# Attention rows written straight into the output projection's input buffer, and the expert scatters spread over seven steps

## The reference

```python
x = x + _layernorm(attn_ref(_layernorm(x), ...))
x = x + _layernorm(ffn_ref(_layernorm(x), ...))
# attn_ref, at its end:
scores = jnp.where(causal, -jnp.inf, einsum('bhqd,bhkd->bhqk', q, k) * scale)
out = einsum('bhqk,bhkd->bhqd', softmax(scores), v)
out = out.transpose(0, 2, 1, 3).reshape(b, s, E)
return out @ wo + bo
# ffn_ref: shared expert of every row, plus w[:, e] * expert e for the top 2 of 8
```

## Time and profile before

| | |
|---|---|
| median of 3 runs | 858.82 us (854.71 to 861.81) |
| the profiled execution | 860.77 us, its span 859.0 us |
| PE / PEld busy | 673.4 / 330.8 us (78% / 39%) |
| DVE / ACT / POOL busy | 611.7 / 502.0 / 322.8 us (71% / 58% / 38%) |
| DMA | 70.38 MB in 110289 packets, 45136 of them under 512 bytes |

### The profile page before, as it was taken

One profiled execution on the slowest core, in us unless ns is written; L12 is line 12 of the kernel. 1 busy time (PEld: TensorE's weight loads), 2 busy tenths in 40 slices (PEclk: granted clock), 3 DMA queues, 4 the chain that ended last, 5 costly groups with the idle time before them and its releaser, 6 DMA issues. The chain is left out here.

```text
span 859.0 us, 17320 instructions
## 1 busy us (share of the span) xinstructions
PE 673.4 (78%) x6080; PEld 330.8 (39%) x6111; DVE 611.7 (71%) x1244; ACT 502.0 (58%) x1048; POOL 322.8 (38%) x437
## 2 busy tenths in 40 slices
PE   5876289999898898988898998795486799989800
PEld 2332023333342242332242343232364677777600
DVE  6999498888878979868979878851246256555466
ACT  3663066777768786768776778684253234444323
POOL 3775012222222331742331742323612436465632
PEclk9998589999999999999999999998687999999955
DMA  5456261121222212422222431012521235232182
GB/s 147 138 171 179 61 165 37 23 53 49 57 52 53 74 53 55 96 70 41 74 62 46 121 71 29 21 54 58 177 74 38 70 87 154 75 84 67 44 226 73
DMA packets 110289, 70.38 MB, mean 82 GB/s; under 512 B 45136, under 2 KB 96753, under 8 KB 110207
## 3 DMA queue, kind: packets, MB, share of 16 engines
q1 hardware_dynamic: 97356, 56.34, 26.4%
q0 software_dynamic: 4352, 8.99, 3.1%
q10 hardware_dynamic: 8498, 3.97, 1.8%
HBM read 40.21 MB, written 26.56 MB: 78 GB/s over the span
## 5 line engine op out<-in xcount | busy, mean ns | idle before, releaser
L1145 ACT ACTIVATE expT<-ps 128x512 f32<-128x512 f32 (+1 forms) x640 | 324.9, 557 | 129.6 <-PE ps L1373 124.4
L303 DVE TENSOR_REDUCE block_max<-ps 128x8 f32<-128x1024 f32 x288 | 340.3, 1218 | 61.8 <-PE ps L288 43.1
L1346 PE MATMUL ps<-expT,vr 128*9 128x256 f32 (+1 forms) x2560 | 180.1, 363 | 17.2 <-ACT oT L1118 14.8
L1373 PE MATMUL ps<-q_space,k_space 64*128 64x512 bf16 (+3 forms) x768 | 164.1, 335 | 10.2 <-DMA q_space<-negT 6.7
L288 PE MATMUL ps<-k_space,q_space 64*128 64x128 bf16 (+3 forms) x1152 | 132.7, 281 | 34.6 <-DVE block_max L303 24.3
L1106 POOL TENSOR_SCALAR_AFFINE_SELECT expT<-expT 128x512 f32<-128x512 f32 x128 | 82.4, 656 | 195.2 <-ACT expT L1145 195.1
L1373 PEld LDWEIGHTS ps<-q_space,k_space 64*128 64x128 bf16 x768 | 46.2, 94 | 150.7 <-ACT expT L1145 99.7
L1555 POOL DMA_INDIRECT expert_rows<-row_ring,tile_to x72 | 68.9, 957 | 69.0 <-ACT row_ring L1639 46.9
L1346 PEld LDWEIGHTS ps<-expT,vr 128*9 128x9 f32 x2560 | 42.3, 89 | 99.3 <-issue 47.5
L715 POOL DMA_INDIRECT sorted_rows<-rows,places x64 | 63.2, 988 | 42.9 <-DVE places L900 25.1
L288 PEld LDWEIGHTS ps<-k_space,q_space 64*128 64x128 bf16 x1152 | 49.7, 96 | 73.9 <-DVE block_max L303 58.2
(11 more groups left out here) (200 smaller groups left out, 949.6 us busy)
## 6 DMA issues: line engine op xcount, KB each, us to landing
row_ring<-sorted_rows SPq DMA_DIRECT2D x72, 65.0 KB, 2.0
q_parts<-parts SPq DMA_DIRECT2D x24, 128.0 KB, 2.3
k_parts<-parts SPq DMA_DIRECT2D x24, 128.0 KB, 2.3
q_space<-q_parts SPq DMA_DIRECT2D x32, 96.0 KB
k_space<-k_parts SPq DMA_DIRECT2D x32, 96.0 KB
v_ones<-v_st SPq DMA_DIRECT2D x8, 288.0 KB, 2.7
vr<-v_ones SPq DMA_DIRECT2D x16, 144.0 KB
q_space<-q_parts SPq DMA_DIRECT2D x32, 64.0 KB
```

What stands on the lines that cost most here:

```text
L303: nc.vector.reduce_max(bm[:, g % 2, 2 * f:2 * f + 2, at:at + 4], ps[:, 2 * odd:2 * odd + 2].rearrange("p h (n k) -> p h n k", k=P), AX_X). ...
L1145: act.activation(expT[:, (NS * g + s) % PTN, hh, 0:width], ps[:, B_S + n % S_RING, 0:width], ACT.Exp, scale=SCALE).then_inc(exp_ok, 1)
L1346: last = nc.tensor.matmul(ps[32 * hh:32 * hh + VW, B_O, at:at + n], vr[:, g % RING, kt, hh * VW:(hh + 1) * VW], expT[:, (NS * g + s) % PTN ...
L1373: last = nc.tensor.matmul(ps[:, B_S + n % S_RING, col:col + m], head_rows(kr, g, hh, slice(kt * P, (kt + 1) * P)), head_rows(qr, g, hh, sl ...
```

## The change

The DRAM tensor `attn` and the buffer `att` go. VectorE's multiply writes its four heads' columns straight into the buffer that `turn_at` reads. That buffer is now double by batch: `at_even` for batches 0 and 2, and `at_odd`, which lies in a part of `q_space` that stage two doesn't use, for batches 1 and 3. `turn_at` waits for VectorE's last multiply of the batch instead of the loads, and `load_chunk` loads only the rows of x. The twelve scatters that stood in steps 3 to 6 of groups 8 and 12 are now seven in steps 3 to 6 of these groups and five in steps 3 to 5 of groups 9 and 13. The number of score banks is three in both kernels.

```diff
+SENT = {(0, 3): (4, 2), (0, 4): (6, 2), (0, 5): (8, 2), (0, 6): (10, 1), (1, 3): (11, 2), (1, 4): (13, 1), (1, 5): (14, 2)}
-        at3 = sb(top, "at3", [P, 2, NT, E])
+        at_even = sb(top, "at_even", [P, 2, NT, E])
+        at_odd = q_space[:, 0, GH // 2:].rearrange("p h s -> p (h s)").bitcast(F32).rearrange("p (c t e) -> p c t e", c=2, e=E)
-        AT_DMAS = NG + 1
+        AT_DMAS = 1
+        def at_rows(c):
+            return (at_even, at_odd)[c // 2 % 2][:, c % 2]
+        def att_ready(c):
+            return used_after("out", NG * (c // 2 + 1) - 1, c % 2)
 def load_chunk(sp, c):
             wait(sp, mid_ok, c - 1)
-            for hg in range(NG):
-                sp.dma_start(at3[:, c % 2, :, hg * GH * HD:(hg + 1) * GH * HD], ad[c // 2, hg, c % 2]).then_inc(at_in[c % 2], DMA)
 def turn_at(pe, c, bank):
-            pe.wait_ge(at_in[c % 2], DMA * AT_DMAS * (c // 2 + 1))
+            pe.wait_ge(wide_used, att_ready(c))
 # SP, stage two
-                        for half in range(2):
-                            sp.wait_ge(att_out[half], DMA * NG * (q + 1))
-                            if at == slot and kind == "out":
-                                sp.wait_ge(wide_used, n + 1)
-                                store(gg, which)
-                sp.wait_ge(att_out[0], DMA * G)
                 load_chunk(sp, CHUNKS - 2)
-                sp.wait_ge(wide_used, used_after("out", G - 1, 1))
-                store(G - 1, 1)
-                sp.wait_ge(att_out[1], DMA * G)
                 load_chunk(sp, CHUNKS - 1)
 # GpSimd, stage two: after root(...) of the same step
-                    if q >= 1 and r == 0 and 3 <= s < 7:
-                        for i in range(3 * (s - 3) + 4, 3 * (s - 3) + 7):
-                            scatter(pool, q - 1, i // PAIR_T, i % PAIR_T)
+                    if q >= 1 and (r, s) in SENT:
+                        rows_sent(q - 1, *SENT[r, s])
 # VectorE, "out"
-                        v.reciprocal(rsum[:, which], o[:, :, HD]).then_inc(recip_ok, 1)
-                        wait(dve, att_out[which], DMA * g)
-                        v.tensor_tensor(att[:, which].rearrange("p t (h d) -> p (t h) d", d=HD), o[:, :, 0:HD],
-                                        rsum[:, which].unsqueeze(2).to_broadcast([P, NT * GH, HD]),
+                        v.reciprocal(r, o[:, :, :, HD]).then_inc(recip_ok, 1)
+                        v.tensor_tensor(at_rows(2 * (g // NG) + which)[:, :, cols_of].rearrange("p t (h d) -> p t h d", d=HD),
+                                        o[:, :, :, 0:HD], r.unsqueeze(3).to_broadcast([P, NT, GH, HD]),
                                         ALU.mult).then_inc(wide_used, 1)
```

More of the change, by code:

```diff
@@ L902, in turn_at @@
         def turn_at(pe, c, bank):
-            pe.wait_ge(at_in[c % 2], DMA * AT_DMAS * (c // 2 + 1))
+            pe.wait_ge(wide_used, att_ready(c))
             for t in range(NT):
-                last = nc.tensor.transpose(ps[:, bank, t * P:(t + 1) * P], at3[:, c % 2, t], identf[:])
+                last = nc.tensor.transpose(ps[:, bank, t * P:(t + 1) * P], at_rows(c)[:, t], identf[:])
             last.then_inc(at_turned, 1)
@@ L971, in block_kernel @@
             recip_ok = sem(two, "recip_ok")
-            att_out = [sem(two, f"att_out{h}") for h in range(2)]
             B_S, S_RING, B_O = 4, 3, 7
@@ L995, in load @@
                     load_group(sp, g)
-                def store(g, half):
-                    sp.dma_start(ad[g // NG, g % NG, half], att[:, half]).then_inc(att_out[half], DMA)
                 def place_neg(g):
@@ L1041, in _ @@
                         for p, _, at, kind, gg, which, n in items:
-                            if at == slot and kind == "out":
-                                sp.wait_ge(wide_used, n + 1)
-                                store(gg, which)
-                            elif at == slot and kind == "neg":
+                            if at == slot and kind == "neg":
                                 sp.wait_ge(wide_used, n + 1)
                                 place_neg(gg)
-                sp.wait_ge(att_out[0], DMA * G)
                 load_chunk(sp, CHUNKS - 2)
-                sp.wait_ge(wide_used, used_after("out", G - 1, 1))
-                store(G - 1, 1)
-                sp.wait_ge(att_out[1], DMA * G)
                 load_chunk(sp, CHUNKS - 1)
@@ L1075, in split_neg, with rows_sent @@
                     nc.gpsimd.tensor_scalar(n[2], left[:], -1.0, None, ALU.mult).then_inc(split, 1)
+                def rows_sent(q, first, n):
+                    for i in range(first, first + n):
+                        scatter(pool, q, i // PAIR_T, i % PAIR_T)
                 def side(g, s):
@@ L1089, in side @@
                     if q >= 0 and r == 3 and s >= 8:
-                        for t in (2 * (s - 8), 2 * (s - 8) + 1):
-                            scatter(pool, q, 0, t)
-                    if q >= 1 and r == 0 and 3 <= s < 7:
-                        for i in range(3 * (s - 3) + 4, 3 * (s - 3) + 7):
-                            scatter(pool, q - 1, i // PAIR_T, i % PAIR_T)
+                        rows_sent(q, 2 * (s - 8), 2)
+                    if q >= 1 and (r, s) in SENT:
+                        rows_sent(q - 1, *SENT[r, s])
                 split_neg(0)
@@ L1204, in item @@
                         dve.wait_ge(wide_ready, n + 1)
[L1205 to L1206 removed]
+                        o = ps[:, 2 * odd].rearrange("p (t h w) -> p t h w", h=GH, w=32)
+                        r = rsum[:, which].rearrange("p (t h) -> p t h", h=GH)
+                        v.reciprocal(r, o[:, :, :, HD]).then_inc(recip_ok, 1)
                         dve.wait_ge(recip_ok, 2 * g + which + 1)
[L1208 to L1210 removed]
+                        cols_of = slice(GH * HD * (g % NG), GH * HD * (g % NG + 1))
+                        v.tensor_tensor(at_rows(2 * (g // NG) + which)[:, :, cols_of].rearrange("p t (h d) -> p t h d", d=HD),
+                                        o[:, :, :, 0:HD], r.unsqueeze(3).to_broadcast([P, NT, GH, HD]),
                                         ALU.mult).then_inc(wide_used, 1)
@@ L1584, in norm_proj @@
                 def norm_proj(c):
-                    normalize(act, 0, c, ps[:, B_PROJ[c % 2]].rearrange("p (t e) -> p t e", e=E), at3[:, c % 2], range(NT))
+                    normalize(act, 0, c, ps[:, B_PROJ[c % 2]].rearrange("p (t e) -> p t e", e=E), at_rows(c), range(NT))
                 A, Z = CHUNKS - 2, CHUNKS - 1
```

10 lines of the change are left out of this document (4 added, 6 removed).

## The result

The changed kernel took **851.9 us** (median of 20 runs, 845.1 to 857.1), the kernel before 858.85 us (20 runs, 854.71 to 863.92). The ratio is 0.9915, 95% interval 0.9896 to 0.9934. That is 7.0 us faster, and 5.7 to 8.9 us by the interval. The forecast was 10.6 us. The two profiled executions do differ by 10.7 us (860.77 and 850.1), as the sum over one profile had said. The medians do not.

A forecast was written before the change was run, and what follows sets the result against it. TensorE was taken to set stage two's pace, with the DRAM trip costing at its reload waits and the stage's end. 4.6 + 5.6 + 0.4 = 10.6 us off the 858.8 median gave 848.2 us, range 843.5 to 853.0.

The forecast's parts named there:

- The wait of `turn_at`: Groups 8 and 12: TensorE's waits for the reload and the clock loss behind one go, 4.6 us gained, lower bound 0.
- rival (b): Stage two: another wait takes the reload's place, only the 6.0 us of the stage's end remain, 852.8 us; chance 0.10.
- The scatters: GpSimd, groups 8, 9, 12, 13: moved scatters cost nothing, with 2.0 us of slack before group 9's split.
- The multiply: VectorE's multiply in its new write form: cost taken as 0, bounded by 9.3 us, with 2 us kept for the range.
- SP's queue: SP in stage two: 32 stores and 32 loads go, nothing waits on the moved loads; costed at nothing.
- The end of the stage: End of stage two: SP no longer last, GpSimd's DRAIN ends it, stage three starts at 598.0; 5.6 us gained.
- The bound of 7.8 us: End of stage two: upper bound of the gain, if VectorE's end decides when stage three starts.
- (a): End of stage two: GpSimd's DRAIN, lengthened by contention with SP's transfers, doesn't hold it; 2.2 us earlier, 846.0 us; chance 0.12.
- (e): End of stage two gives nothing, SP being held elsewhere: 854.2 us; chance 0.04.
- The start of stage three: First rows come sooner by 0 to 2 us; only ScalarE's wait for the first down product counts, 0.4 us.
- Rival (c): TensorE's clock falls differently after the shorter gap: 1.5 us a stretch, two make 851.2 us; high side's chance 0.08.

The follow-up runs named there:

- the down weights first: The kernel before with SP's down weight loads ahead of its last store and reload (chunk 7): 858.85 us, ratio 0.9981.
- scatters alone: The kernel before with only the new places of the twelve scatters, attention rows still through DRAM: 861.82 us, ratio 1.001.
- the kernel without late scatters: The changed kernel with group 15's four scatters moved to the start of stage three, second chip: 879.87 us, ratio 0.9861 to the kernel before.
- the kernel with early roots: The changed kernel, stage three's four roots between and right behind its scatters, ahead of the row numbers: 875.76 us (second chip), 847.93 us (third).

## Why the prediction was right, and where it was off

The sum of waits, by trace, in us. The kernel before has three traces: the first, the one on the third chip, and the one with the scatters moved (which changes nothing that can be told). The changed one has four: the first, two more, and the one with the scatters moved back.

| | before | after | mean difference |
|---|---|---|---|
| group 8 | 31.41, 28.62, 31.04 | 27.84, 27.84, 27.84, 27.97 | -2.5 |
| group 12 | 29.09, 28.89, 28.65 | 27.84, 27.84, 27.84, 27.96 | -1.0 |
| the gap | 8.05, 8.09, 7.98 | 2.35, 2.80, 2.80, 1.92 | -5.6 |
| groups 14 and 15, to VectorE's end | 61.8, 63.2, 61.6 | 61.5, 65.2, 62.5, 64.5 | +1.2 |
| stage three to the expert tiles | 83.5, 81.0, 81.9 | 82.9, 84.2, 84.2, 78.8 | +0.4 |

With +0.2 for what is left (stage one, groups 0, 7 and 11, the tiles) this adds up to -7.3 us, and the spans of these traces differ by 7.2 by mean; the medians of the first comparison differ by 7.0. That the first pair of traces gave the forecast's 10.6 us almost to the tenth is luck: the before one had the longest of the three group 8s and the after one no stretch at 1.2 GHz in group 15.

- **The wait of `turn_at`, 4.6 us: the mechanism was right, the size was off.** The wait is gone and no other took its place, which refutes rival (b). But 2.0 us of wait and 1.5 us of the clock were what one execution showed. In four traces with the DRAM trip (these three and the down weights first) the waits of the two groups add up to 1.6 to 4.3 us, and the stretch at 1.2 GHz doesn't always follow. The term measured 3.5 us. This is the first of the two steps that failed: a race between a DMA and TensorE was costed from one execution that had lost it by much.
- **My reason beside it was not borne out.** I took group 4, which has neither wait nor scatters, for a hint that scatters had part in the wait. With seven scatters in place of twelve the wait stayed (1.7 and 0.8 us). The traces offer another reason: in group 4 the turn comes 24.4 us after the group's start, for 22.5 us in group 8, while the reload is issued at about the same place, so it has 2 us more. Nothing was run that sets the two apart.
- **The scatters, 0: right**, and for the reason given. The split of group 9 is still released by VectorE's join, with 2.37 us to spare where 2.0 was worked out; groups 9 and 13 took 31.9 us in both kernels; scatters alone gave 1.001. By the Trainium skill's rule of the shared SBUF interfaces (GPSIMD Engine Reference, Key points) the slack could have gone; beside VectorE's one-input work the five scatters of group 9 took 0.96 to 1.04 us each, so it didn't bear here, and the rule itself wasn't tested.
- **The multiply, 0: right** (291 ns, as before). **SP's queue, 0: right**; nothing waits for a later `place_neg`.
- **The end of the stage, 5.6 us: right** in size (5.6 by mean) and in who is last. The bound of 7.8 us was not reached, because GpSimd's DRAIN ends after VectorE's, and rivals (a) and (e) fell with it. The reason given against (a) was wrong, though: 3.0 us is not what a scatter takes to land. The row numbers of stage three find the last scatter landed 1.4 to 1.5 us after it ends, and the DRAIN has nearly the same tail (2.70 us) with no scatter near it. The term came out because the tail is the same in both kernels, not because it was understood. That the term needed the trace of what was hidden is the point of it: on the page of before nothing speaks of GpSimd at that place.
- **The start of stage three, 0.4 us.** The rows came 1.6 us sooner (3.4 us for 5.0). The Trainium skill (DMA: Bandwidth & Descriptors, Latency and other measured facts) puts the fixed cost of a DMA at about 2 us; the 3.4 us that are left don't contradict it, and no run here splits it from the transfer and the queue. The first root comes 17.30 us after the stage's start, for 17.65, but that is one scatter's time (the longest of the twelve took 1.40 us before and 1.02 after) and not the rows. The 0.4 us of the forecast does not show: this stretch is 0.4 us longer by mean, and it spreads by 5 us.
- **What the sum left out, +1.2 us or so: the second step that failed.** Rival (c) took a stretch at 1.2 GHz more as one case with a price of 1.5 us at the side. Such stretches turn up in group 15 in three of the four traces of the changed kernel and in one of the three of the kernel before. With them groups 14 and 15 take 62.5 to 65.2 us, without them 61.5 to 61.8. Whether the change brings them or chance does, seven traces can't settle, and it stays open.
- **The numbers.** The time lay in the range. The chance of 0.65 for faster by over 1% followed from the 10.6 us; at 7 us (0.7 to 1.0%) "within 1%" was the case that came.

## What to carry to other kernels

Cost a wait that is a race between a transfer and an engine from several executions, or give it half: one profile shows one outcome of it, and a difference of two profiles can flatter the forecast (10.7 us here for 7.0 of the medians). Before removing the last engine's work at a barrier, read the ends of all engines' DRAINs, since the next one decides the gain; here it was GpSimd's, whose tail grew with the indirect DMAs of its block. The cheap step after the change (four scatters moved past the barrier, roots taken in front of scatters) was worth 9.5 us, more than the change. Scatters queued on an in-order engine cost nothing beside slack and cost much beside small pieces that others wait for, so set the small pieces first.

## What the runs showed of the hardware that was not expected

- The tail of GpSimd's DRAIN, from the end of its last instruction to the DRAIN's own end, goes with the number of indirect DMAs that GpSimd has issued in the block, whenever that was. In the fourteen traces it is 0.07 us at the end of stage one (none), 2.70 us at the end of stage two with 32 of them, 3.01 us with 36, 8.25 us at the end of stage three with 100 and 8.57 us with 104, each to 0.01 us. In stage three the last of them is over 30 us back. The last root of the changed kernel and the DRAIN behind it, with SP's, and then the same DRAIN of the kernel without late scatters:

```profile
838.46 1.42 POOL L1531 TENSOR_TENSOR out_rstd<-out_var_eps,neghalf 128x4 f32<-128x4 f32 x1 [2.13 <-DVE out_var_eps L1673]
...
L1385 POOLq DRAIN  x1: 9699/9699/9699, 838.4 to 838.4; - x1
...
L1385 SPq DRAIN  x1: 7/7/7, 845.1 to 845.1; - x1
```

```profile
L1385 POOLq DRAIN  x1: 10027/10027/10027, 866.6 to 866.6; - x1
```

That is an estimate of 0.08 us for each indirect DMA (5.23 us over 64 of them, 0.31 and 0.33 us over four); the cause wasn't found. So an earlier place for a scatter within the block doesn't shorten the tail, but fewer of them do. The same tail ends the kernel: in the changed kernel GpSimd's DRAIN ends at 848.1, 3.0 us after SP's, the next to last. No run tried to shorten it.
- On the second chip, the other engines stand still beside scatters in a row. In the kernel with early roots there, VectorE sits still until the sixth is over (VectorE's timeline and then GpSimd's, group 8):

```profile
365.19 0.26 DVE L1204 RECIPROCAL rsum<-ps 128x16 f32<-128x16 f32 x1 [6.22 <-remote]
```

```profile
357.84 0.97 POOL L723 DMA_INDIRECT sorted_rows<-rows,places  x1 [0.16 <-issue]
...
364.17 0.96 POOL L723 DMA_INDIRECT sorted_rows<-rows,places  x1 [0.30 <-issue]
```

In the kernel without late scatters VectorE goes on during the fifth, after 4.6 us. Groups 8 and 12 take about 35 and 36 us there, for 27.84 us on the two other chips with the same instructions, and 28.1 and 28.7 us with their scatters moved to groups 9 and 13. The kernel before is 32 us slower on that chip as well, of which no trace was taken. What in that chip does it was not found.
- The same kernel's executions spread by 12 us (845.1 to 857.1), and the mean granted clock goes with it: 0.940 in the fastest, 0.917 in the slowest.
